# Setup stage of a two-layer transformer kernel: modulation as rows, and the input and first weights loaded inside it

## The reference, cut to what matters

```
mod = silu(c) @ wmod                     # (1, 1536): six vectors of 256
shift_a, scale_a, gate_a, shift_f, scale_f, gate_f = split(mod, 6)
h = layernorm(x) * (1 + scale_a) + shift_a
x = x + g(gate_a) * mixer(h)             # g: the sign of the gate times max(|gate|, 0.25)
```

## Time and profile before

| | |
|---|---|
| median of 3 runs | 3164.16 us (3161.39 to 3174.41) |
| the profiled execution's own time | 3166.68 us |
| its span, from first to last instruction | 3164.9 us |
| mean granted TensorE clock | 0.911 of full speed |
| PE busy | 2700.3 us (85%) |
| DVE busy | 2272.9 us (72%) |
| ACT busy | 1580.0 us (50%) |
| DMA, mean | 41 GB/s |

### The profile page before, as it was taken

One profiled execution on the slowest core, in us unless ns is written; L12 is line 12 of the kernel. 1 busy time (PEld: TensorE's weight loads), 2 busy tenths in 40 slices (PEclk: granted clock), 3 DMA queues, 4 the chain that ended last, 5 costly groups with the idle time before them and its releaser, 6 DMA issues. The chain is left out here.

```text
span 3164.9 us, 91211 instructions
## 1 busy us (share of the span) xinstructions
PE 2700.3 (85%) x35152; PEld 1676.1 (53%) x35152; DVE 2272.9 (72%) x4338; ACT 1580.0 (50%) x2158; POOL 374.9 (12%) x341
## 2 busy tenths in 40 slices
PE   4896999989999998999999975999987777319997
PEld 3331366646665665566566623555545555207765
DVE  1547889878888887988899912656556887675676
ACT  0330377766676676776777772111116666204442
POOL 0228000000000000000000010000001122202333
PEclk7995799999999999999999987999998887659998
DMA  3226011011101111011110001000000222313331
GB/s 105 80 80 114 2 26 21 10 26 26 26 13 17 26 26 27 5 25 25 26 26 6 5 4 49 27 27 13 13 2 22 70 77 84 109 29 104 111 106 57
DMA packets 130635, 130.30 MB, mean 41 GB/s; under 512 B 76418, under 2 KB 107780, under 8 KB 125060
## 3 DMA queue, kind: packets, MB, share of 16 engines
q1 hardware_dynamic: 124548, 120.93, 16.2%
q10 hardware_dynamic: 4224, 4.19, 0.4%
q0 software_dynamic: 1536, 0.40, 0.1%
HBM read 78.41 MB, written 46.66 MB: 40 GB/s over the span
## 5 line engine op out<-in xcount | busy, mean ns | idle before, releaser
L646 DVE TENSOR_REDUCE attn_pm<-attn_MS 128x1 f32<-128x512 f32 (+3 forms) x2304 | 1335.8, 640 | 224.0 <-PE attn_MS L690 196.8
L630 ACT ACTIVATE attn_PT<-attn_ES 128x1024 f32<-128x1024 f32 (+5 forms) x1152 | 1039.2, 951 | 399.1 <-PE attn_ES L725 396.2
L690 PE MATMUL attn_MS<-attn_KX,attn_QX 96*32 96x512 bf16 (+10 forms) x9216 | 1054.0, 376 | 7.1 <-DVE attn_pm L646 5.6
L725 PE MATMUL attn_ES<-attn_QX,attn_KX 99*32 99x512 bf16 (+6 forms) x9216 | 784.9, 363 | 72.8 <-issue 32.0
L740 PE MATMUL attn_OP<-attn_PT,attn_VH 128*17 128x512 f32 (+2 forms) x4608 | 660.7, 566 | 9.3 <-issue 9.1
L690 PEld LDWEIGHTS attn_MS<-attn_KX,attn_QX 96*32 96x32 bf16 x9216 | 415.7, 97 | 289.4 <-issue 116.6
L725 PEld LDWEIGHTS attn_ES<-attn_QX,attn_KX 99*32 99x32 bf16 x9216 | 383.2, 98 | 217.5 <-issue 63.8
L740 PEld LDWEIGHTS attn_OP<-attn_PT,attn_VH 128*17 128x17 f32 x4608 | 193.8, 99 | 62.0 <-issue 15.6
L1100 PE MATMUL l0out_ring<-l0out_w,l0out_sT 128*128 128x512 f32 x512 | 225.0, 592 | 0.0
L685 PE MATMUL attn_MS<-attn_maskb,identb 128*32 128x128 bf16 (+3 forms) x2048 | 172.8, 207 | 38.5 <-DMA attn_QX<-qk_parts 25.7
L578 POOL TENSOR_SCALAR attn_parts<-attn_nmT 32x128 bf16<-32x128 f32 x16 | 22.6, 1411 | 1424.6 <-DVE attn_nmT L655 1424.6
(11 more groups left out here) (272 smaller groups left out, 2985.1 us busy)
## 6 DMA issues: line engine op xcount, KB each, us to landing
attn_KX<-qk_parts SPq DMA_DIRECT2D x96, 128.0 KB, 6.4
attn_QX<-qk_parts SPq DMA_DIRECT2D x96, 128.0 KB, 7.0
vk_beta<-front_vk SPq DMA_DIRECT2D x8, 1024.0 KB, 3.9
kq_transposed<-front_qkG SPq DMA_DIRECT2D x8, 1024.0 KB, 4.5
delta_VK<-vk_beta SPq DMA_DIRECT2D x32, 256.0 KB, 2.8
delta_QK<-kq_transposed SPq DMA_DIRECT2D x32, 256.0 KB, 2.9
attn_out<-attn_OS SPq DMA_DIRECT2D x128, 34.0 KB
x_res<-in_L_attn_x_dram ACTq DMA_DIRECT2D x8, 512.0 KB, 9.4
```

The costliest lines, as they stand in the source:

```text
L630: nc.scalar.activation(PT[u % NPT][:, 512 - wa:512 + wb], ES[half][:, 512 - wa:512 + wb], ACT.Exp, scale=DH ** -0.5).then_inc(exp_done, 1)
L646: nc.vector.tensor_reduce(pm[r][:, i, c:c + 1], MS[slot][:, 0:w], AX.X, ALU.max).then_inc(max_taken, 1)
L690: last = nc.tensor.matmul(MS[slot][r, 0:seen], QX[b][0:ROWS, i * P + 32 * g:i * P + 32 * g + 32], KX[b][0:ROWS, 512 * c:512 * c + seen], s ...
L725: last = nc.tensor.matmul(ES[half][r, o + past:o + w], KX[b][0:MAXR, kt * P + 32 * g:kt * P + 32 * g + 32], QX[b][0:MAXR, a + past:a + w], ...
```

## The change

- `setup` is called with x_res, the first weights' tiles and their semaphores, which are now made in `build`. The first weights and biases lie in `w2` (a tile that a later stage fills), by way of `project_weights`. `project` uses these and issues none of the loads any more.
- SP issues the eight weight and bias loads right behind the five loads of `setup`. ACT issues the eight loads of x after the two silu activations and ahead of its new copies.
- TensorE computes rows alone: three products of 512 columns for each layer and half, 12 products in all, with a semaphore step after each pair. It starts when the first layer's `silubc` is ready.
- ACT and DVE copy the rows out as they come. Five vectors are needed as columns as well or alone; they are copied as three lines of 512 in one partition (`line`), and TensorE turns them to columns with 12 products of one partition by one column (`k["ones"][0:1, 0:1]`). It waits for two steps of ACT, one more of ACT and one of DVE first.
- The gates are formed by layer: the first layer's two while TensorE is still at the second layer, the second layer's two at the end.

The diff, cut to its core:

```
+def project_weights(w2):
+    flat = w2[:].rearrange("p h e n -> p (h e n)")
+    wqk = flat[:, 0:EH * 2 * E].rearrange("p (h i n) -> p h i n", h=EH, i=2)
+    wvh = flat[:, EH * 2 * E:EH * (3 * E + HID)].rearrange("p (h n) -> p h n", h=EH)
+    end = EH * (3 * E + HID)
+    return wqk, wvh, flat[:, end:end + 4], flat[0:1, end + 4:end + 4 + E + HID]
...
         @block.sync
...
+            wqk, wvh, bqk, bvh = first_weights
+            for dst, name in ((wqk[:, :, 0, :], "Wq"), (wqk[:, :, 1, :], "Wk"), (wvh[:, :, 0:E], "Wv"),
+                              (wvh[:, :, E:], "dp_w1")):
+                sp.dma_start(dst, d[f"L0_attn_{name}"].rearrange("(h p) n -> p h n", p=P)).then_inc(wl, 16)
...
         @block.scalar
...
             last.then_inc(silu_done, 1)
+            xv = d["L0_attn_x"].rearrange("o (t p) c -> p (o t) c", p=P)
+            for g in range(G):
+                act.dma_start(x_res[:, J * g:J * g + J, :], xv[:, J * g:J * g + J, :]).then_inc(xl, 16)
+            act.wait_ge(rows_done, 1)
+            nc.scalar.activation(line[:, 0, :], rowp[0:1, 0, :], ACT.Copy).then_inc(line_done, 1)
+            act.wait_ge(rows_done, 2)
+            nc.scalar.activation(line[:, 1, 0:E], rowp[0:1, 1, E:], ACT.Copy)
+            nc.scalar.activation(raw[:, 0, :], rowp[:, 1, 0:E], ACT.Copy).then_inc(a_copied, 1)
+            act.wait_ge(rows_done, 4)
+            nc.scalar.activation(line[:, 2, :], rowp[0:1, 3, :], ACT.Copy).then_inc(line_done, 1)
+            act.wait_ge(rows_done, 5)
+            nc.scalar.activation(raw[:, 2, :], rowp[:, 4, 0:E], ACT.Copy).then_inc(a_copied, 1)
+            nc.scalar.activation(k["sb1"][:], rowp[:, 4, E:], ACT.Copy)
...
         @block.vector
...
+                last.then_inc(bc_done, 1)
+            def gates(l):
+                two = slice(2 * l, 2 * l + 2)
...
+            dve.wait_ge(rows_done, 3)
+            nc.vector.tensor_copy(line[:, 1, E:], rowp[0:1, 2, 0:E]).then_inc(v_copied, 1)
+            nc.vector.tensor_copy(raw[:, 1, :], rowp[:, 2, E:]).then_inc(v_copied, 1)
+            dve.wait_ge(a_copied, 1)
+            dve.wait_ge(v_copied, 2)
+            gates(0)
+            dve.wait_ge(rows_done, 6)
+            nc.vector.tensor_scalar(k["cb1"][:], rowp[:, 5, 0:E], 1.0, None, ALU.add)
+            nc.vector.tensor_copy(raw[:, 3, :], rowp[:, 5, E:]).then_inc(v_copied, 1)
+            dve.wait_ge(cols_done, 1)
             for l in (0, 1):
+                for at, plus in ((0, 0.0), (2, 1.0), (6, 0.0), (8, 1.0))[:4 - 2 * l]:
+                    nc.vector.tensor_scalar(k[f"mod{l}"][:, at:at + 2], colp[:, 12 * l + at:12 * l + at + 2],
+                                            plus, None, ALU.add)
+            dve.wait_ge(a_copied, 2)
+            dve.wait_ge(v_copied, 3)
+            gates(1)
...
         @block.tensor
         def _(pe):
-            pe.wait_ge(v_done, 1)
             for l in (0, 1):
-                for m in range(12):
+                pe.wait_ge(bc_done, l + 1)
+                for n in range(3):
                     for h in range(EH):
-                        nc.tensor.matmul(colp[:, l, m:m + 1], wm[l][:, h, m * P:(m + 1) * P],
-                                         k[f"silu{l}"][:, h:h + 1], start=(h == 0), stop=(h == 1))
-            for i, (l, w) in enumerate(rows):
-                for h in range(EH):
-                    last = nc.tensor.matmul(rowp[:, i, 0:E], k[f"silubc{l}"][:, h, :],
-                                            wm[l][:, h, w * E:(w + 1) * E], start=(h == 0), stop=(h == 1))
-            last.then_inc(mm_done, 1)
+                        last = nc.tensor.matmul(rowp[:, 3 * l + n, :], k[f"silubc{l}"][:, h, :],
+                                                wm[l][:, h, 2 * n * E:2 * (n + 1) * E], start=(h == 0), stop=(h == 1))
+                    last.then_inc(rows_done, 1)
+            pe.wait_ge(line_done, 2)
+            pe.wait_ge(a_copied, 1)
+            pe.wait_ge(v_copied, 1)
+            for l, n, at in ((0, 0, 0), (0, 1, 6), (1, 2, 0)):
+                for m in range(4):
+                    last = nc.tensor.matmul(colp[:, 12 * l + at + m:12 * l + at + m + 1],
+                                            line[:, n, m * P:(m + 1) * P], k["ones"][0:1, 0:1], start=True, stop=True)
+            last.then_inc(cols_done, 1)
```

More of the change, by code:

```diff
@@ L43, in bcast, with setup @@
     return ap.rearrange("(o c) -> o c", o=1).broadcast_to([n, ap.shape[0]])
-def setup(nc, k, d, sb, sem):
+def project_weights(w2):
[4 more added lines that the diff above has]
+    return wqk, wvh, flat[:, end:end + 4], flat[0:1, end + 4:end + 4 + E + HID]
+def setup(nc, k, d, sb, sem, x_res, first_weights, xl, wl):
     ld = sem("loaded_weights")
@@ L71, in setup @@
         raw = st.enter_context(nc.sbuf_tensor("rawrow", [P, 4, E], F32))
-        colp = st.enter_context(nc.psum_tensor("colp", [P, 2, 512], F32))
+        line = st.enter_context(nc.sbuf_tensor("modline", [1, 3, 2 * E], F32))
+        colp = st.enter_context(nc.psum_tensor("colp", [P, 512], F32))
         rowp = st.enter_context(nc.psum_tensor("rowp", [P, 6, 512], F32))
-        silu_done, mm_done, v_done, id_done = sem("silu_done"), sem("modmm_done"), sem("mod_done"), sem("id_done")
+        silu_done, bc_done, id_done = sem("silu_done"), sem("silu_broadcast"), sem("id_done")
+        rows_done, line_done, cols_done = sem("modrows_done"), sem("modline_done"), sem("modcols_done")
+        a_copied, v_copied, v_done = sem("rows_copied_act"), sem("rows_copied_dve"), sem("mod_done")
         block = st.enter_context(nc.Block())
-        rows = [(0, 2), (0, 5), (1, 2), (1, 5), (1, 4), (1, 3)]
         @block.sync
@@ L83, in _ @@
             load(sp, k["ident"][:], d["c_ident"])
+            wqk, wvh, bqk, bvh = first_weights
+            for dst, name in ((wqk[:, :, 0, :], "Wq"), (wqk[:, :, 1, :], "Wk"), (wvh[:, :, 0:E], "Wv"),
+                              (wvh[:, :, E:], "dp_w1")):
+                sp.dma_start(dst, d[f"L0_attn_{name}"].rearrange("(h p) n -> p h n", p=P)).then_inc(wl, 16)
+            for i, name in enumerate(("bq", "bk")):
+                sp.dma_start(bqk[:, 2 * i:2 * i + 2], d[f"L0_attn_{name}"].rearrange("(h p) -> p h", p=P),
+                             allow_slow_non_contiguous=True).then_inc(wl, 16)
+            sp.dma_start(bvh[:, 0:E], d["L0_attn_bv"].rearrange("(o n) -> o n", o=1)).then_inc(wl, 16)
+            sp.dma_start(bvh[:, E:], d["L0_attn_dp_b1"].rearrange("(o n) -> o n", o=1)).then_inc(wl, 16)
         @block.gpsimd
@@ L105, in _ @@
                                                    k[f"silu{l}"][:, h:h + 1], None, ALU.mult)
-            last.then_inc(v_done, 1)
-            dve.wait_ge(mm_done, 1)
-            for l in (0, 1):
[L109 to L128, removed]
+                last.then_inc(bc_done, 1)
+            def gates(l):
+                two = slice(2 * l, 2 * l + 2)
+                n = 4 * l
+                nc.vector.tensor_scalar(tmp[:, two, :], raw[:, two, :], 0.0, 2.0, ALU.is_ge, ALU.mult).then_inc(v_done, 1)
+                dve.wait_ge(v_done, n + 1)
+                nc.vector.scalar_tensor_tensor(raw[:, two, :], raw[:, two, :], -1.0, raw[:, two, :],
+                                               ALU.mult, ALU.max).then_inc(v_done, 1)
+                nc.vector.tensor_scalar(tmp[:, two, :], tmp[:, two, :], -1.0, None, ALU.add).then_inc(v_done, 1)
+                dve.wait_ge(v_done, n + 3)
+                for i, name in enumerate((f"ga{l}", f"gb{l}")):
+                    last = nc.vector.scalar_tensor_tensor(k[name][:], raw[:, 2 * l + i, :], 0.25, tmp[:, 2 * l + i, :],
+                                                          ALU.max, ALU.mult)
+                last.then_inc(v_done, 1)
@@ L149, in project @@
+            last.then_inc(cols_done, 1)
+def project(nc, k, d, sem, x_res, v17, HD, qk_dram, first_weights, xl, wl):
     FV = Steps("stats", "aggr", "rstd", "xn")
@@ L2437, in build @@
         AF = w2[:].rearrange("p h e (i x) -> p (h e i) x", x=C).rearrange("p (c i) x -> p c i x", c=CT)
+        xl, wl = sem("x_loaded"), sem("w1_loaded")
+        first_weights = project_weights(w2)
+        setup(nc, k, d, sb, sem, x_res, first_weights, xl, wl)
         with ExitStack() as first:
@@ L2448, in build @@
                 parts = [qk_parts[i] for i in range(3)]
-                project(nc, k, d, sem, x_res, v17, HD, parts)
+                project(nc, k, d, sem, x_res, v17, HD, parts, first_weights, xl, wl)
                 attention(nc, k, d, sem, v17, parts, ot, gate, issue0, scale0)
```

18 lines of the change are left out of this document (1 added, 17 removed).

## The result

The changed kernel takes 3086.80 us (median of 4, 3081.95 to 3087.55), the kernel before 3166.15 in the runs beside it. The ratio is 0.9735, with a 95% interval of 0.9715 to 0.9755. It is faster by 79 us; I had forecast 32 to 33, in a range whose lower end was 3123. The forecast is wrong: 45 us come from stages that the change doesn't name.

What follows compares the result with a forecast made beforehand. A serial head up to DVE's start on x was taken as the bound; moving that start from 66.11 to 33.0 us saves 33.1, giving 3133.6 from the profiled run or 3131.1 from the median. Forecast 3132 us, range 3123 to 3144.

Steps and rivals of the forecast that it cites:

- Start of PE: In setup, PE starts at 13.96 us, after the five loads land at 13.12 and the first two silubc are made.
- the rival: In setup, the eight queued loads make the first five land 3.1 us later, giving 3134 us; chance 14%.
- Rows: In setup, PE's 24 row instructions of 512 columns end at 26.6 us, bounds 26.1 and 27.2.
- ACT's issues: In setup, issuing the eight loads of x occupies ACT's queue for 9.45 us, leaving ACT free at 22.9.
- Columns: In setup, PE's 24 one-column instructions take 3.3 us and are done at 29.9.
- DVE's end and the stage change: Setup ends at 32.6 us after DVE's copies and gates; with 0.27 for the change, project starts at 32.9.
- Table load: In project, ACT's square root table load runs from 32.9 to 34.2 us, hidden by 0.8 beside DVE's statistics.
- the first part: Opening account of what bounds the kernel: the chain up to DVE's start on x, with 3098.8 us behind it unchanged.
- The rival that looked behind project: Attention's clock goes another way after the earlier start: gain mostly or wholly lost 4%, or slower, 3180 us, 2%.
- The last sign under what would show it: The prediction is wrong if the stretch behind the statistics changes its length by over 10 us.
- the cases below 3148: All outcomes but gain lost later (4%) and slower (2%); below 3148 us counts as faster, given 0.95.

Runs made afterwards that it cites:

- early shift of 143: Changed kernel with 143 unused semaphore increments ahead of PE's first wait in setup, moving all its later code: 3150.1 us, ratio 0.9914.
- shift of 113 in the kernel before: Kernel before the change with 113 unused semaphore increments ahead of PE's first wait in setup: 3123.5 us, ratio 0.9838.
- 143 at the head of attention: Changed kernel with 143 unused semaphore increments at the head of PE's list in attention, moving only attention and later code: 3139.6 us, ratio 0.9898.
- without the head loads: Kernel before the change with the K and Q loads of heads 3 to 15 left out, their semaphore raised instead: 3120.6 us, ratio 0.9840.
- shift of 256 instructions: Changed kernel with 256 unused semaphore increments at the head of PE's list in attention: 3103.5 us, ratio 0.9798.

## Why the prediction was wrong

The steps of setup held. In the order of the prediction:

- *Start of PE* at 13.96: 14.15. The five loads landed at 13.26 for 13.12, so the eight behind them cost 0.1 us at most, of the 3.1 that the rival had.
- *Rows* to end at 26.6: 26.13 (14.15 + 11.98). The quicker spacing came 3.2 us after the first of them, a little ahead of my 3.5 to 5.6.
- *ACT's issues* over at 22.9: 21.2. The first line was copied at 21.28, and PE never waited for it.
- *Columns* 3.3 us: 2.83, each instruction 0.12 us. The granted clock was 1.00 from 26.06 to 28.90. An instruction with one partition of weights was hardly cheaper than the 0.13 us of a transpose with 128.
- *DVE's end and the stage change* at 32.9: the last gate ended at 31.62, the statistics began at 32.14. x did not hold them.
- *Table load* from 32.9, hidden by 0.8 us: it began at 33.10, since ACT waits for POOL's memset of v ahead of it (L252 of before), which I had overlooked, and ended at 34.38, 0.3 us after the statistics' hand-over (33.72 + 0.38). The Trainium skill (ScalarE: Activation LUTs, What ACT_TABLE_LOAD costs) adds 1.38 us of drain. The trace disagrees here: the memset ended at 32.93, the load ran from 33.10 to 34.38, and the square root starts at 34.40.

The start of the statistics came to 34.0 us for 33.1. What failed is one sentence of the first part: "what lies behind it, 3098.8 of the span's 3164.9 us, stays as it is". It became 3053.6, and 36.2 of these 45.2 us lie in the attention scores: 27.1 as shorter idle times of PE and 9.1 as busy time at a higher mean clock. The runs put this down to the position of PE's code, most of it against the burst of loads. I took instructions removed from setup as removed from setup alone. The rows that would have told were there: PE's idle times of up to 8.5 us that end with "issue", in a stage that I read only as windows of busy time and clock. The rival that looked behind project went by the clock and only the losing way, with the bound that "they start from the same semaphores, data and gaps as before"; the gaps were not the same. The last sign under what would show it, a stretch behind the statistics that changes by over 10 us, is the one that came true. (The chances had a small slip too: the cases below 3148 add to 94%, for the 95% given to faster.)

Two of the smaller terms are likely of the same kind but not shown apart: the 3.8 us of layer 1's front came back with the early shift of 143 (469.2 us), and were absent with the shift of 113 in the kernel before (465.5); with the 143 at the head of attention only 1.7 us of them came back (467.1). The 2.3 us of project lie within what that stage does on its own: 288.1, 285.1 and 283.5 in three kernels with the same project code. The 2.4 us at the end did not come back with the early shift of 143 (316.5) and stay unexplained.

How an instruction packet is held up is shown in part. The trace records each packet of q8. In the stall of the kernel before that begins at 646.97, the packet started 4.49 us after PE's last product had ended, took 1.78 us, and PE went on 1.91 us after its end. The DMA view from 651.4 to 653.3 us has it beside the data:

```profile
q1 hardware_dynamic: 52, 0.21, 94.2%
q8 instruction: 1, 0.02, 5.9%
```

In the same stall without the head loads (638.38 to 641.70) the three parts were 0.74, 0.95 and 1.64 us. So of the 4.9 us that the burst adds to this stall, 3.75 pass before the packet starts, 0.8 are its own slower transfer and 0.3 lie behind it. In the third long stall (1246.47 to 1254.37) two packets stood one behind the other, from 1248.55 to 1250.30 and from 1250.56 to 1252.22.

What holds the packet back ahead of its start isn't shown. The Trainium skill (DMA: Bandwidth & Descriptors, Queues, rings and completion order) says that a DMA engine takes turns between its queues packet by packet, and that such a packet is a group of typically about 9 to 17 descriptors. In this trace the data of the burst are 190 entries of 8 KB between 643 and 656 us, at 1.01 us each on average, and 174 of 4 bytes. If one such entry is one descriptor, a packet of 9 to 17 of the large ones would occupy its engine for some 9 to 17 us, an estimate from the page's count and the 1.01 us. The measured 4.5 us would fit into such a turn; no run here shows where the packets of that rule begin and end.

## What to carry to other kernels

A program that streams its instructions from memory has its own code as one more transfer: where a burst of loads fills the DMA engines while an engine runs through unrolled code, look for idle times that end with "issue", and spread the burst. An edit that changes the number of instructions of an engine moves all its later code; so ahead of crediting or blaming an edit for a stage it doesn't touch, shift the code by a fraction of a packet and back by a whole one, and see what of the result follows. Here such shifts were worth 40 to 51 us with the burst, more than what the change was made for (34).

## What was unexpected of the hardware

- The duration of an untouched stage depended on the instruction count ahead of it: 1515 to 1520 us at one position, 1555 to 1570 at another, with the first again after a shift of 256 instructions.
- A semaphore increment on PE took 0.15 us of its time, so 143 of them didn't fit under 14 us of idleness.
- One load of 256 four-byte elements held SP's queue for 4.49 us when issued behind 4 MB of other loads (bq, at 5.74), where it took 0.60 before; the like load of bk right behind it took 0.54. Nothing waited for it here.
- The long stalls of PE each had a 16 KB instruction packet inside them. In the one that was compared, most of the wait that the burst added lay before that packet started (3.75 of 4.9 us), not in its transfer.
